# Counts of destinations taken ahead of the normalisation, and rank products placed behind 20 projection tiles instead of 30, in the sort stage of a graph-attention kernel

## Chip, cores and metric

The kernel runs on one core of a Trainium2 chip, as one program. The metric is the device time of one execution in microseconds (us). The kernel before takes 4097.71 us, the median of three runs (4089.75 to 4097.94).

## The reference, cut to what matters

Four layers run one after another over 6250 nodes and 106250 edges that come sorted by destination; the hidden width is 256.

```
x = x + gnn0(layernorm(x), src, dst, edge_attr)   # attention over edges, 8 heads
x = x + ffn0(layernorm(x))                        # sliced attention over nodes
x = x + gnn1(layernorm(x), src, dst)
x = x + moe(layernorm(x))                         # 8 experts, the best 2 for each node
```

The change touches only the stage ahead of the first layer. It finds where each node's edges begin in the sorted list (a count of the entries of `dst` below the node's number), orders the nodes by the number of their edges, and computes the first layer's projection of the normalised nodes, `layernorm(x) @ W.T` with 16 more columns of attention scores.

## The kernel before

`sort_nodes` is the first stage. Its 6250 nodes are 50 tiles of 125. Every engine has a list of instructions that it works off in order; engines wait for each other on semaphores. The stage ends with a barrier for all engines (the block begins at L259), and the next stage, `windows`, starts behind it.

**Counting, in two steps.** `dst` is cut into 250 blocks of 425 edges. TensorE counts for every node how many blocks begin below it (L518). `index(g)` (L349) turns the counts of 10 tiles into block numbers. GpSimd then gathers, tile by tile, the one block in which each node's first edge lies (L338): 125 rows of 425 integers, 212.5 KB, into a ring `drow` of R = 10 buffers. `count(t)` (L355) waits until gather t has landed, and counts the entries below each node; it frees the buffer (`used`). So gather t + 10 waits for `count(t)`, and for the `index` of its group of ten.

**VectorE's order (L358 to L399).** `index(0)`; a wait for the weights (`w_in`, L365); 25 tiles of the layernorm's statistics (`norm.tile`, L375); `index(1)` to `index(4)`; `count(0)` to `count(9)`; the other 25 statistics (L381); the variances; two copies that make the edge records `rec` (L385, L386); `norm.scales` (L388); `count(10)` to `count(49)`; then the starts of all nodes `rpf`, their degrees and a one-hot of the degrees, `hot` (L399).

**Projection, three engines and SyncE's queue.** For each tile ScalarE normalises (`xn`, L484), TensorE transposes (`turn`, L529) and multiplies (`product`, L538), ScalarE copies the result into one of RB = 5 buffers `row` (L496), and SyncE issues four DMAs that write it to `rows0` and `own0` (L282, L283). ScalarE's copy of tile t waits until tile t - 5 has been written. `product(t)` waits until row t - 2 has been copied. SyncE first waits for the edge records (`rec_made`, L268), writes them and four small zero rows, then issues 30 tiles, then a copy of the whole of `x` into `own0` (L288), then the other 20 tiles.

**Ranks.** `ranks()` (L547) is two products for each of 7 column blocks; VectorE copies each block out (L403, L404) before TensorE may write the next. TensorE's list is: ten tiles as `group(0)`, `group(1)`, `group(2)`, then `ranks()`, then `group(3)`, `group(4)`, then ten `place(g)` (L557), which need VectorE's one-hots `at_q`, `at_t` and `vals` (L423 to L427). Some small vector work on the result (L430 to L466) ends the stage.

Of the kernel before, what the change touches and what calls it, by code (L numbers as in the profile page):

```python
# [25 lines left out]
NT = N // P  # L26
# [136 lines left out]
def sort_nodes(nc, K, ins, dr):  # L163


    with ExitStack() as stack:
        m = Mem(nc, stack)
        J, R, RB, W, GT, PG, B = 2, 10, 5, 10, 10, 5, 2
# [90 lines left out]
        with nc.Block() as block:  # L259
# [85 lines left out]
            def _(dve):  # L345
# [3 lines left out]
                def index(g):  # L349
                    ts = slice(g * GT, (g + 1) * GT)  # L350
                    dve.wait_ge(counted, (g + 1) * GT)
                    v.tensor_scalar(blk_i[:, ts], pN[g], -1.0, 0.0, ALU.add, ALU.max).then_inc(idx_ok, 1)
                    v.tensor_scalar(blk[:, ts], pN[g], -1.0, 0.0, ALU.add, ALU.max)

                def count(t):  # L355
                    dve.wait_ge(landed[t % R], 16 * (t // R) + 16)
                    return v.tensor_scalar(drow[:, t % R, :], drow[:, t % R, :], node[:, t:t + 1], 0.0, ALU.is_lt, ALU.add, accum_out=cnt[:, t:t + 1]).then_inc(used, 1)
# [3 lines left out]
                for j in range(J):  # L361
                    v.tensor_scalar(below[:, j, :], iota_n, dst0f[:, j:j + 1], None, ALU.is_gt).then_inc(below_ok, 1)
                index(0)

                dve.wait_ge(w_in, 64)  # L365
                dve.wait_ge(consts, 3)
# [6 lines left out]
                half = NT // 2  # L373
                for t in range(half):
                    norm.tile(v, t, x[:, t:t + 1, :])  # L375
                for g in range(1, NT // GT):
                    index(g)
                for t in range(R):
                    count(t)
                for t in range(half, NT):  # L380
                    norm.tile(v, t, x[:, t:t + 1, :])  # L381
# [4 lines left out]
                v.tensor_copy(rec[:, :, 1:4], attrw[:]).then_inc(rec_made, 1)  # L386
                dve.wait_ge(sq, 1)
                norm.scales(v, ch, rst)  # L388
                for t in range(R, NT):
                    count(t)  # L390
                dve.sem_inc(used, 1)
                dve.wait_ge(used, NT + 1)
# [117 lines left out]
            @block.tensor  # L510
            def _(pe):
                t_ = nc.tensor
                bl = below[:].rearrange("p j (n t) -> p j t n", t=NT)
                pe.wait_ge(consts, 1)
                pe.wait_ge(below_ok, J)
                for t in range(NT):
                    for j in range(J):
                        last = t_.matmul(pN[t // GT][:, t % GT:t % GT + 1], bl[:, j, t, :], ones[:], start=(j == 0), stop=(j == J - 1))  # L518
                    last.then_inc(counted, 1)
                pe.wait_ge(ablk_ok, 1)  # L520
                for i in range(2):
                    for k in range(2):
                        last = t_.matmul(pW[:, i, 0:2 * H], wn[:, k, i * 128:(i + 1) * 128], ablk[:, k, :], start=(k == 0), stop=(k == 1))
                last.then_inc(wa_ok, 1)

                def turn(t, b):
                    pe.wait_ge(xn_ok, t + 1)
                    for k in range(2):
                        last = t_.transpose(pT[b][:, k, 0:P], xn[:, b, k * 128:(k + 1) * 128], K["ident"][0:P, 0:P])  # L529
                    last.then_inc(t_ok, 1)  # L530

                def product(t, b, early):
                    pe.wait_ge(xnT_ok, t + 1)
                    if not early:
                        pe.sem_inc(pace, 1)
                        pe.wait_ge(row_ok, t - 1)
                    for k in range(2):
                        last = t_.matmul(pH[b][:, 0:D + 2 * H], xnT[:, b, k, :], wx[:, k, :], start=(k == 0), stop=(k == 1))  # L538
                    last.then_inc(h_ok, 1)

                def group(u, first, last_group):
                    for r in range(W):
                        if r < W - 1 or not last_group:
                            turn(W * u + (r + 1), (r + 1) % 2)
                        product(W * u + r, r % 2, first and r < 2)

                def ranks():  # L547
                    pe.wait_ge(hot_ok, 1)
                    for j, (a, b) in enumerate(cols):
                        h = wide[:, a * NB:b * NB]  # L550
                        w = (b - a) * NB
                        if j:
                            pe.wait_ge(taken, j)
                        t_.matmul(pR[0:P, 0:w], K["tri"][0:P, 0:P], h, start=True, stop=True)
                        t_.matmul(pTt[:, 0:w], K["ones"][0:P, 0:P], h, start=True, stop=True).then_inc(mm_ok, 1)

                def place(g):  # L557
                    pe.wait_ge(hot2, g + 1)
                    for i in range(PG):
                        last = t_.matmul(pR[:, 0:3 * QT], at_q[:, g % B, i, :], vals[:, g % B, i, :, :].rearrange("p k t -> p (k t)"),  # L560
                                         start=(g == 0 and i == 0), stop=(g == NT // PG - 1 and i == PG - 1))
                    last.then_inc(placed, 1)
                pe.wait_ge(wx_ok, 1)
                turn(0, 0)
                group(0, True, False)
                group(1, False, False)
                group(2, False, False)
                ranks()
                group(3, False, False)
                group(4, False, True)  # L570
                for g in range(NT // PG):
                    place(g)
                pe.wait_ge(deg_ok, 1)
                t_.transpose(pD[0:QT, :], K["deg"][:], K["ident"][:]).then_inc(dT_ok, 1)
                pe.wait_ge(cnt_ok, 1)
                t_.matmul(pC[:, 0, 0:QT + 1], cf[:], K["tri"][0:QT, 0:QT + 1], start=True, stop=True)
                t_.matmul(pC[:, 1, 0:QT + 1], wf[:], K["tri"][0:QT, 0:QT + 1], start=True, stop=True)
                t_.matmul(pC[:, 1, QT + 1:QT + 2], none[:], K["ones"][0:QT, 0:1], start=True, stop=True)
                t_.matmul(pC[:, 1, QT + 2:QT + 3], shallow[:], K["ones"][0:QT, 0:1], start=True, stop=True)
                t_.matmul(pC[:, 2, 0:QT], c8[:], K["ident"][0:QT, 0:QT], start=True, stop=True)  # L580
                t_.matmul(pD[:, 0:QT], K["ones"][0:QT, :], diag[:], start=True, stop=True).then_inc(pre_ok, 1)
# [1600 lines left out]
```

## Time and profile before

| | |
|---|---|
| time, median of 3 runs (range) | 4097.71 us (4089.75 to 4097.94) |
| profiled execution: time | 4103.11 us |
| profiled execution: span, first to last instruction | 4101.4 us |
| busy share of the span: TensorE, VectorE, ScalarE, GpSimd | 73%, 56%, 31%, 56% |
| mean granted TensorE clock | 0.876 of full speed |
| end of the sort stage (the next stage's first instruction on GpSimd) | 238.67 us after the span's start |

The sort stage is the first 239 us of the span. The busy shares are averages over many stages with other limits, so what is said here is read from the stage's own stretch of the trace: the list of waits, the instructions in order of time, and the landing of transfers.

### The profile page before, as it was taken

To read this page: it belongs to the slowest core of one execution; us is meant where nothing else is said; L and a number is where in the kernel's file an instruction comes from. 1 tells how busy PE (TensorE), PEld (TensorE's weight loads), DVE (VectorE), ACT (ScalarE), POOL (GpSimd) and SP (SyncE) were. 2 spreads that over 40 slices of the span, in tenths; PEclk is the share of its full clock that TensorE was granted. 3 is DMA by queue.
4 is the path that set the end of the run, shared out by engine and by line. 5 is a ranking of instruction groups with operands and counts; after the bars stand their busy time and mean duration, and the time that the engine had idled before them with its cause. 6 is when DMAs were issued, how large, how long until landed. Compare 5 with 4: busy or idle time off the path is not lost. (4 is left out here: it accounts for less than half of the span.)

```text
span 4101.4 us, 69475 instructions
## 1 busy us (share of the span) xinstructions
PE 2992.8 (73%) x12787; PEld 2170.0 (53%) x12788; DVE 2302.0 (56%) x5192; ACT 1264.3 (31%) x5387; POOL 2289.2 (56%) x2343
## 2 busy tenths in 40 slices
PE   4632777787788777998666565566556489999998
PEld 3421444444444444667544444444444379998987
DVE  4532888888888887874355555555555621111111
ACT  1401444444445454432211111111111233433333
POOL 5156777777777773001477777777777523333332
PEclk9966899999999999998778877777787699999999
DMA  8636444344444443000244444444444756666664
GB/s 185 195 89 163 105 106 105 104 107 109 109 109 110 111 112 70 0 2 27 72 112 114 113 112 113 113 113 112 113 113 112 218 151 175 169 174 167 177 168 131
DMA packets 292185, 487.94 MB, mean 119 GB/s; under 512 B 145315, under 2 KB 193393, under 8 KB 291625
## 3 DMA queue, kind: packets, MB, share of 16 engines
q0 software_dynamic: 127312, 325.41, 32.3%
q1 hardware_dynamic: 155936, 158.55, 13.2%
q10 hardware_dynamic: 8880, 3.34, 0.4%
q8 instruction: 21, 0.34, 0.0%
q14 instruction: 36, 0.29, 0.0%
HBM read 430.09 MB, written 57.50 MB: 119 GB/s over the span
## 5 line engine op out<-in xcount | busy, mean ns | idle before, releaser
L893 POOL DMA_INDIRECT g_rows<-rows,g_recs x1856 | 1760.1, 948 | 643.3 <-issue 469.1
L933 PE MATMUL g_pA<-g_msg,k_ident 128*128 128x264 f32 (+1 forms) x3712 | 1140.7, 460 | 476.3 <-DVE g_pA L1122 418.9
L933 PEld LDWEIGHTS g_pA<-g_msg,k_ident 128*128 128x128 f32 x3712 | 800.0, 227 | 801.3 <-issue 659.5
L922 PE MATMUL g_pE<-g_ew,g_recT 128*128 128x512 f32 x932 | 508.6, 672 | 251.2 <-DVEq L1106 248.8
L1116 DVE TENSOR_TENSOR g_msg<-g_rows,g_pp 128x1024 f32 (+3 forms) x464 | 572.0, 1233 | 155.5 <-DVEq L84 155.4
L1962 POOL DMA_INDIRECT out<-e_ys,e_goal x102 | 160.6, 1575 | 490.5 <-issue 466.1
L922 PEld LDWEIGHTS g_pE<-g_ew,g_recT 128*128 128x128 f32 x932 | 169.8, 202 | 468.5 <-DVEq L1106 343.0
L2015 PE MATMUL e_pY<-e_w,e_hT 128*128 x1632 | 375.1, 383 | 19.5 <-issue 19.0
L2004 PEld LDWEIGHTS e_pH<-e_xT,e_w 128*128 128x128 f32 x3264 | 382.6, 193 | 5.1
L2004 PE MATMUL e_pH<-e_xT,e_w 128*128 128x128 f32 x3264 | 382.9, 276 | 0.0
L1041 ACT ACTIVATE g_pp<-g_dd 128x32 f32<-128x32 f32 x464 | 95.2, 205 | 919.3 <-ACTq L84 919.3
L2100 DVE TENSOR_TENSOR e_ys<-e_pY,k_x 128x256 f32<-128x256 f32 x102 | 43.4, 425 | 573.6 <-PE e_pY L2015 573.6
L2015 PEld LDWEIGHTS e_pY<-e_w,e_hT 128*128 128x128 f32 x1632 | 302.5, 190 | 68.9 <-issue 31.8
L1149 DVE TENSOR_REDUCE g_al<-g_prod 128x32 f32<-128x1088 f32 x232 | 297.1, 1281 | 56.4 <-DVEq L84 56.4
L1101 DVE SCALAR_TENSOR_TENSOR g_prod<-g_pE,g_dall 128x1024 f32<-128x1024 f32 x232 | 283.4, 1221 | 18.5 <-DVEq L84 7.3
L1055 ACT ACTIVATE g_pA<-g_pA,g_cs 128x33 f32<-128x33 f32 x1464 | 276.4, 277 | 4.4
L2057 ACT ACTIVATE e_hT<-e_pH,e_b 128x128 f32<-128x128 f32 x816 | 221.6, 382 | 43.1 <-issue 40.5
L2044 ACT ACTIVATE e_xT<-e_pX,e_bl,e_gl 128x128 f32<-128x128 f32 x204 | 82.2, 453 | 494.5 <-PE e_pX L1987 494.5
L994 ACT ACTIVATE g_recT<-g_pRT 16x128 f32<-16x128 f32 x234 | 62.2, 266 | 557.1 <-ACTq L84 556.9
L1153 DVE TENSOR_TENSOR g_al<-g_rows,k_sdst 128x32 f32 (+1 forms) x232 | 44.8, 193 | 287.1 <-DVEq L84 282.3
L1544 POOL MEMSET f_bu<- 128x16 f32 x1 | 0.1, 112 | 287.3 <-POOLq L113 287.3
L1949 POOL DMA_INDIRECT e_xs<-tok,e_at x102 | 100.4, 984 | 71.5 <-DVE e_at L2110 35.1
(418 smaller groups left out, 3467.6 us busy)
## 6 DMA issues: line engine op xcount, KB each, us to landing
e_w<-in_L_ffn_W SPq DMA_DIRECT2D x110, 1024.0 KB
g_rows<-rows,g_recs POOLq DMA_INDIRECT x1856
g_recs<-slots SPq DMA_DIRECT2D x468, 8.0 KB
tok<-e_xall SPq DMA_DIRECT2D x7, 910.0 KB
rows<-p_row SPq DMA_DIRECT2D x50, 119.0 KB
own<-p_row SPq DMA_DIRECT2D x50, 119.0 KB
p_x<-in_x SPq DMA_DIRECT2D x1, 5600.0 KB
own<-p_x SPq DMA_DIRECT2D x1, 5600.0 KB
```

Source lines behind the costliest of these rows:

```text
L893: pool.indirect_dma_start(out=rows[:, r, j, :], out_offset=None, in_=rows_d, in_offset=bass.IndirectOffsetOnAxis(ap=recs[:, r, 4 * j:4 * j ...
L922: last = t_.matmul(pE[:, c:c + 512], recT[:], ew[:].rearrange("p c d -> p (c d)")[:, c:c + 512], start=True, stop=True)
L933: last = t_.matmul(sums, K["ident"][:], of, start=False, stop=(j == C - 1), skip_group_check=True)
L1055: last = s.activation(of[:, h, :], of[:, h, :], ACT.Copy, scale=cs[:, h:h + 1])
L1101: v.scalar_tensor_tensor(to, pE[:].rearrange("p (c h w) -> p c h w", c=C, h=H), 0.0, over(by_head(own), 1, C), ALU.max, ALU.mult).then_inc ...
L1116: v.tensor_tensor(to, of, by, ALU.mult).then_inc(msg_ok, 1)
L1149: ch.link(v.reduce_sum(sc, prod[:], axis=AX))
L1949: pool.indirect_dma_start(out=xs[:, b, :], out_offset=None, in_=dr["tok"], in_offset=bass.IndirectOffsetOnAxis(ap=at[b][:, 0:1], axis=0)). ...
L1962: pool.indirect_dma_start(out=out, out_offset=bass.IndirectOffsetOnAxis(ap=goal_b[b][:, 0:1], axis=0), in_=ys[:, b, :], in_offset=None, bo ...
L2004: last = t_.matmul(pH[b][c][:, j, :], w1[:, b, k, units], xT[:, b, k, :], start=(k == 0), stop=(k == 1))
L2015: last = t_.matmul(pY[b][:], hT[:, b, k, :], w2[:, bass.ds(e, 1), k, :].rearrange("p a h -> p (a h)"), start=(k == 0), stop=(k == KC - 1))
L2057: last = s.activation(hT[:, b, c * HK + j, :], pH[b][c][:, j, :], ACT.Gelu, bias=b1[:, bass.ds(e, 1), c * HK + j])
```

## The change

VectorE's `index(1)` to `index(4)` and `count(0)` to `count(13)` go ahead of the wait for the weights, in four portions. `count(14)` to `count(23)` stand between the two halves of the statistics, where `count(0)` to `count(9)` stood. The rest, `count(24)` to `count(49)`, stays behind `norm.scales`. On TensorE `ranks()` goes ahead of `group(2)`. No instruction is added or taken away.

```diff
@@ -361,6 +361,16 @@
                 index(0)
+                index(1)
+                for t in range(4):
+                    count(t)
+                index(2)
+                for t in range(4, 7):
+                    count(t)
+                index(3)
+                index(4)
+                for t in range(7, 14):
+                    count(t)
 
                 dve.wait_ge(w_in, 64)
                 dve.wait_ge(consts, 3)
@@ -373,9 +383,7 @@
                 half = NT // 2
                 for t in range(half):
                     norm.tile(v, t, x[:, t:t + 1, :])
-                for g in range(1, NT // GT):
-                    index(g)
-                for t in range(R):
+                for t in range(14, 24):
                     count(t)
                 for t in range(half, NT):
                     norm.tile(v, t, x[:, t:t + 1, :])
@@ -386,7 +394,7 @@
                 norm.scales(v, ch, rst)
-                for t in range(R, NT):
+                for t in range(24, NT):
                     count(t)
@@ -564,8 +572,8 @@
                 group(0, True, False)
                 group(1, False, False)
+                ranks()
                 group(2, False, False)
-                ranks()
                 group(3, False, False)
                 group(4, False, True)
```

## Rows read from the trace of the kernel before

**Rows 1.** Waits in the sort stage: engine, line, waited for, us, times, longest.

```profile
ACT p_row L496 <- DMA own<-p_row: 45.8, 28, 10.0
DVE p_ablk L367 <- DMA p_wx<-in_L_gnn_WT: 31.1, 1, 31.1
DVE o_at_q L423 <- PE o_pR L560: 16.6, 1, 16.6
```

**Rows 2.** Waits of SyncE's own queue, sort stage.

```profile
SPq L270 <- DVE p_rec L386: 73.6, 1, 73.6
SPq L259 <- PEq L259: 13.3, 1, 13.3
```

**Rows 3.** TensorE in order of time: start, us, instruction.

```profile
121.26 1.15 PE L538 MATMUL o_pH<-p_wx,o_xnT 128*125 128x272 f32 x4
...
142.16 1.02 PE L554 MATMUL o_pR<-p_wide,k_tri 125*125 125x512 f32 x2
...
209.30 1.15 PE L538 MATMUL o_pH<-p_wx,o_xnT 128*125 128x272 f32 x4 [0.43 <-ACT o_xnT L489]
210.29 2.68 PE L560 MATMUL o_pR<-o_vals,o_at_q 125*128 125x147 f32 x20
```

**Rows 4.** SyncE's DMA issues in order of time.

```profile
113.83 0.32 SPq L282 DMA_DIRECT2D rows<-p_row  x1
...
131.89 0.32 SPq L282 DMA_DIRECT2D rows<-p_row  x1
...
151.64 0.32 SPq L282 DMA_DIRECT2D rows<-p_row  x1
...
153.68 16.49 SPq L288 DMA_DIRECT2D own<-p_x  x2
...
207.10 0.32 SPq L283 DMA_DIRECT2D own<-p_row  x1
...
222.74 0.32 SPq L283 DMA_DIRECT2D own<-p_row  x1
```

**Rows 5.** VectorE in order of time.

```profile
59.96 0.65 DVE L357 TENSOR_SCALAR_CACHE_REDUCE p_drow<-p_drow,p_node 125x425 int32<-125x425 int32 x1
...
65.72 8.25 DVE L135 BATCH_NORM_STATS2 p_st<-p_x 125x6 f32<-125x256 f32 x25
...
78.89 0.65 DVE L357 TENSOR_SCALAR_CACHE_REDUCE p_drow<-p_drow,p_node 125x425 int32<-125x425 int32 x1
...
131.04 0.66 DVE L357 TENSOR_SCALAR_CACHE_REDUCE p_drow<-p_drow,p_node 125x425 int32<-125x425 int32 x1 [1.02 <-DMA p_drow<-in_dst,p_blk_i]
...
135.62 3.49 DVE L399 TENSOR_TENSOR p_wide<-o_bkt,k_iota 125x3200 f32<-125x3200 f32 x1
...
194.71 0.41 DVE L426 TENSOR_TENSOR o_vals<-o_at_t,o_deg 125x245 f32<-125x245 f32 x1
```

**Rows 6.** GpSimd's gathers 3, 9, 10 and 49 in order of time.

```profile
24.42 1.21 POOL L338 DMA_INDIRECT p_drow<-in_dst,p_blk_i  x1 [0.30 <-issue]
...
33.45 1.21 POOL L338 DMA_INDIRECT p_drow<-in_dst,p_blk_i  x1 [0.30 <-issue]
61.52 1.20 POOL L338 DMA_INDIRECT p_drow<-in_dst,p_blk_i  x1 [26.86 <-DVE p_drow L357]
...
124.14 1.20 POOL L338 DMA_INDIRECT p_drow<-in_dst,p_blk_i  x1 [0.30 <-DVE p_drow L357]
```

**Rows 7.** DMA issues, gathers 3, 9 and 19 alone: last number us to landing.

```profile
p_drow<-in_dst,p_blk_i POOLq DMA_INDIRECT x1, 29.0
...
p_drow<-in_dst,p_blk_i POOLq DMA_INDIRECT x1, 23.9
...
p_drow<-in_dst,p_blk_i POOLq DMA_INDIRECT x1, 5.3
```

**Rows 8.** ScalarE's copy of tile 30, the first behind the ranks.

```profile
166.82 0.40 ACT L496 ACTIVATE p_row<-o_pH 125x272 f32<-125x272 f32 x1 [0.69 <-PE o_pH L538]
```

**Rows 9.** Windows: stretch, length, busy of PE, PEld, DVE, ACT, POOL, clock, DMA share, GB/s.

```profile
142.00:165.30 23.30, 12.46 (x30) 4.53 (x29) 10.29 (x12) 2.08 (x5) 0.00 (x0) 1.00 0.69 204
```

## The prediction

> **What bounds the kernel now.** The page's busy shares don't answer this: they are means over ten stages. The change lies in the sort stage, and the next stage starts behind a barrier, at 238.67 us. So the question is what ends the sort stage last, and I read its waits first, then the order of time on each engine that they point to.
>
> The waits hold two surprises. VectorE does sit idle for 31.1 us early on, until the weights land; but late in the stage it also waits 16.6 us for TensorE's placement products [rows 1]. VectorE had made the inputs of the first two placements by 195.12 (194.71 + 0.41) [rows 5], and TensorE began them only at 210.29, straight behind the product of tile 49, which started at 209.30 [rows 3]. The chain of counts therefore has 15 to 17 us to spare before the end: making it shorter makes that wait longer. The projection sets the end.
>
> What sets the projection? ScalarE's copies of the rows wait 45.8 us in 28 times for the writes of rows before them [rows 1], and those are issued by SyncE. Its queue hardly pauses: a tile takes four issues, 2.04 us from the last tile at 151.64 to the copy of x at 153.68, and the last write is issued at 222.74 [rows 4]. The list of its own waits has one long entry before it starts, the edge records (73.6 us), and one after it ends, 13.3 us at the barrier [rows 2]. Product 49 needs row 47, row 47's buffer needs tile 42 written, and tile 42's last issue is at 207.10 [rows 4], 2.2 us before the product. So the path is: the statistics and the records on VectorE, SyncE's queue to tile 42, product 49, placements, the small vector work. The stretch from the first placement to the barrier is 28.4 us (238.67 - 210.29) and does not change.
>
> Two questions are left. Does the change move the start of SyncE's queue? Does it make that queue run dry?
>
> **The early counts: the start.** The gathers that the early counts wait for share the transfer engines with the load of x. Gather 3, started at 24.42, took 29.0 us to land: 53.42 [rows 6, 7]. That hides now behind the wait for the weights, whose end lets the statistics start. In the changed order count 3 comes before that wait, and ten buffers bind everything that follows. Before, gather 10 started 1.56 us after the start of count 0 (59.96 to 61.52) [rows 5, 6]. So gather 13 starts at 53.42 + 1.56 = 54.98. GpSimd needs 1.505 us for each gather ((33.45 - 24.42) / 6 [rows 6]), so gather 23, ten later, starts at 54.98 + 15.05 = 70.03. Gather 19, issued when x had long landed, took 5.3 us [rows 7]; so gather 23 lands at 75.3. Count 23 stands ahead of the second half of the statistics, and a count takes 0.58 us (ten from 59.96 to 65.72 [rows 5]): that half starts at 75.9, where it started at 65.72. **Term 1: +10.2 us** for the second half and for all behind it: variances, records, scales, SyncE's first row.
>
> Nothing earlier on VectorE binds more tightly: gather 13 lands at about 60.3, so the weights' wait is reached at about 61, the first half of the statistics takes 8.25 us as the second does [rows 5], and counts 14 to 22 are taken as they land. The weights ended the old wait at about 51 (59.96 less 8.25 for the first half and about 1 for what lies around it), and could come ten us later without a change. Nor is the removal of the four `index` calls from their old place worth anything, as VectorE waits for gathers there.
>
> Bounds: if gather 3 landed as fast as gather 19, there would be no delay (a rival below); if it landed with gather 9, at 33.45 + 23.9 = 57.35 [rows 6, 7], the term would be 14.1.
>
> The Trainium skill (DMA: Bandwidth & Descriptors, "Anatomy of one DMA") puts a GpSimd-issued transfer at about 2.0 us plus its bytes over 436 GB/s. By that estimate gather 23's 212.5 KB would take 2.5 us, term 1 would be 7.4 and the sum 19.7; the trace's 5.3 us disagrees, and is used.
>
> **The ranks behind 20 tiles: the queue runs dry.** The ranks hold TensorE, and no row is made meanwhile. Before, they started at 142.16, behind tile 29, and the next row was written at 167.22 (166.82 + 0.40) [rows 3, 8], 25.06 us later. This stood where SyncE issued its stock of rows and then the copy of x, an issue of 16.49 us [rows 4]: the hole was covered. Behind tile 19 there is no such cover. In the clock of the old trace TensorE starts product 19 at 121.26; the product before the ranks started 0.99 us ahead of them (product 49 stood as far ahead of the placements [rows 3]), so ranks would start at 122.25 and row 20 would be ready at 147.31. SyncE was ready for tile 20 at 131.89 at the latest [rows 4]. **Term 2: 147.31 - 131.89 = +15.4 us** in which the queue stands still. It can't win that back: behind it lie the same thirty tiles and the copy of x.
>
> This adds to term 1, as both TensorE and SyncE are moved by it alike. Does TensorE wait for the one-hot as well? Count 24 starts where count 10 did, at 78.89 [rows 5], plus 10.2: 89.1. It frees gather 34 (89.1 + 1.56 = 90.65), and 15 more gathers start gather 49 at 113.2; with the last gather's 6.9 us (124.14 to 131.04) its count starts at 120.1, where it was 131.04. The one-hot ended 8.07 us after that start (135.62 + 3.49) [rows 5, 6]: 128.2. TensorE reaches the ranks at about 122.25 + 10.2 = 132.4, later. So no third wait, with some 3 us to spare.
>
> Bounds: below, TensorE alone needs 12.46 us for the ranks [rows 9], if VectorE's copies cost nothing: term 2 would be 25.06 - (23.30 - 12.46) - 9.64 = 4.6, where 9.64 is the stock (131.89 - 122.25). Above, if the last count came no earlier than 131.04, the one-hot would be ready at 139.1, 6.7 us after TensorE: 22.1. The middle value is taken, as the same instructions take the same turns.
>
> **What the gathers give back.** From 113.83 (tile 12) to 153.68, 18 tiles took 39.85 us; at the 2.04 us of the last of them they would take 36.7 [rows 4]. The gathers ran until 131 in that stretch. In the new order they have landed by 121, when tile 12 starts at about 124. **Term 3: -3.1 us**; the other bound is nothing.
>
> **Sum.** 10.2 + 15.4 - 3.1 = +22.5 us. The profiled execution's 4103.11 (span 4101.4 and 1.7 around it) becomes 4125.6. That execution is 5.4 us above the median of the runs, so on their footing it is 4097.7 + 22.5 = 4120.2, rounded to 4120, 0.55% slower. All later stages start behind the barrier and only shift.
>
> **The rivals.**
>
> *The count chain sets the end (faster).* The mechanism would be VectorE's: the last count comes 10.9 us sooner, so ranks and placements do. It decides if placements wait for VectorE and not for product 49. The new time would be 4097.7 - 10.9 = 4087, and SyncE's 13.3 us at the barrier would allow it [rows 2]. Against it stands the wait of 16.6 us in the other direction [rows 1]. 0.05.
>
> *It does nothing (same).* The early gathers land fast enough to leave the statistics where they are, and the hole in TensorE's rows is hidden by rows in stock. 4098. Against it: 29.0 us to land [rows 7] and five buffers, of which 9.64 us of issuing were left. 0.06.
>
> *Only the queue's hole.* Gathers 0 to 3 land early, term 1 is gone: 4097.7 + 15.4 - 3.1 = 4110. 0.06.
>
> *Only the late start.* ScalarE or TensorE is further ahead of SyncE at tile 20 than it was, and term 2 is gone or cut to its low bound: 4097.7 + 10.2 - 3.1 = 4105, or 4109 with the low bound's 4.6. 0.05.
>
> **How the numbers follow.** The forecast, both terms, has 0.78; its own range is 4112 to 4130: terms 1 and 2 together 8 us smaller, or 10 us larger, as with term 1 at its high bound (+3.9) and term 2 near its own (+6.7). The range that should hold 8 in 10 reaches down into the two half cases: 4107 to 4131. No change is what lies within 0.2%, 8.2 us, about what this kernel's runs can tell (their own spread is 8.2). Slower: 0.78 + 0.06 + 0.05 = 0.89; the same 0.06; faster 0.05.
>
> **What would show it.** In the new profile: the second half of the statistics starts near 76; SyncE's first issues come 10 us later; the ranks start near 132 and SyncE's issues stand still for about 15 us behind tile 19; the one-hot is ready a few us ahead of TensorE; VectorE's wait for the first placement grows from 16.6 us to some 50; the placements begin near 233 and the next stage near 262. I would be wrong if gather 3 landed long before 53, if SyncE's issues ran on behind tile 19, or if product 49 were no longer what the placements follow.

## The result and the profile after

The changed kernel takes 4118.46 us, the median of five runs (4116.0 to 4119.18), against 4094.72 for the kernel before (five runs, 4089.75 to 4097.94): a ratio of 1.0057, with a 95% interval of 1.0046 to 1.0068. It is 23.7 us slower; the forecast was 22.5.

The sort stage accounts for nearly all of it. The next stage begins on GpSimd at 260.86 us; before, it began at 238.67, so the stage is 22.2 us longer. The two profiled executions differ by only 12.9 us in span, 4114.3 against 4101.4: behind the sort stage the one of before took 3862.7 us and the one of after 3853.4, with the same work. The delay is not won back in the layers that follow: a load of the last layer on SyncE's queue (tile `e_br`) is issued at 3203.54 before and at 3227.05 after, still 23.5 us late. Only behind that is the execution of after 10.6 us shorter. The six experiments below took 3859.8 to 3863.1 us behind the sort stage, so the 3853.4 stands alone, and its cause is not known. The stage's own end and the timed medians are what to compare.

The waits of the stage come first: engine and line, what was waited for, us in total, times, longest. From the records on, the changed file's lines lie 8 further down.

```profile
ACT p_row L504 <- DMA own<-p_row: 56.3, 22, 27.5
DVE o_at_q L431 <- PE o_pR L568: 51.5, 1, 51.5
DVE p_drow L357 <- DMA p_drow<-in_dst,p_blk_i: 44.1, 21, 18.2
```

```profile
SPq L270 <- DVE p_rec L394: 85.2, 1, 85.2
...
SPq L259 <- PEq L259: 13.2, 1, 13.2
SPq L282 <- ACT p_row L504: 11.9, 1, 11.9
```

The second list is SyncE's own queue. Two entries answer to [rows 2]: the wait for the records grew from 73.6 to 85.2 us, and a wait of 11.9 us for a row is new. The 31.1 us that VectorE spent on the weights [rows 1] are gone from the list, but they are not filled with work: VectorE now waits there for the gathers instead (18.2 us ahead of count 0, 29.5 us in all up to count 13). Its waits for gathers were 27.2 us in the whole stage before, and are 44.1 now. The row of before:

```profile
DVE p_drow L357 <- DMA p_drow<-in_dst,p_blk_i: 27.2, 26, 4.7
```

Its wait for the placement products grew from 16.6 to 51.5 us: the chain of counts got shorter, and handed the time on to that wait.

VectorE in order of time shows the late start:

```profile
53.25 0.66 DVE L357 TENSOR_SCALAR_CACHE_REDUCE p_drow<-p_drow,p_node 125x425 int32<-125x425 int32 x1 [2.20 <-DMA p_drow<-in_dst,p_blk_i]
...
62.17 0.66 DVE L357 TENSOR_SCALAR_CACHE_REDUCE p_drow<-p_drow,p_node 125x425 int32<-125x425 int32 x1 [0.34 <-DMA p_drow<-in_dst,p_blk_i]
...
63.51 8.25 DVE L135 BATCH_NORM_STATS2 p_st<-p_x 125x6 f32<-125x256 f32 x25
71.68 0.64 DVE L357 TENSOR_SCALAR_CACHE_REDUCE p_drow<-p_drow,p_node 125x425 int32<-125x425 int32 x1
...
77.43 8.26 DVE L135 BATCH_NORM_STATS2 p_st<-p_x 125x6 f32<-125x256 f32 x25
...
124.79 3.49 DVE L407 TENSOR_TENSOR p_wide<-o_bkt,k_iota 125x3200 f32<-125x3200 f32 x1
```

Count 3 starts at 53.25, when gather 3 lands; count 13 at 62.17; only then does VectorE come to the weights, for which it no longer waits, and to the first half of the statistics. The second half starts at 77.43, 11.7 us later than in [rows 5].

SyncE's queue in order of time, tiles 0, 19 and 20 and the copy of x:

```profile
97.90 0.35 SPq L282 DMA_DIRECT2D rows<-p_row  x1
...
140.80 0.32 SPq L282 DMA_DIRECT2D rows<-p_row  x1
...
155.10 0.32 SPq L282 DMA_DIRECT2D rows<-p_row  x1
...
177.17 16.52 SPq L288 DMA_DIRECT2D own<-p_x  x2
```

Behind tile 19 there is a hole: a tile takes some 2.07 us, yet tile 20 is issued 14.3 us after tile 19. Against [rows 4] tile 20 and the copy of x are both 23 us late (23.2 and 23.5): nothing is won back. TensorE shows why the hole is there, and where it ends:

```profile
128.91 1.14 PE L546 MATMUL o_pH<-p_wx,o_xnT 128*125 128x272 f32 x4
129.89 1.02 PE L562 MATMUL o_pR<-p_wide,k_tri 125*125 125x512 f32 x2
...
153.27 1.08 PE L546 MATMUL o_pH<-p_wx,o_xnT 128*125 128x272 f32 x4
...
232.87 2.69 PE L568 MATMUL o_pR<-o_vals,o_at_q 125*128 125x147 f32 x20
```

Product 19, the ranks, then product 20 only at 153.27; the placements begin at 232.87, 22.6 us later than in [rows 3].

### The profile page after: what moved, and what is told of

Same layout as the page of the kernel before. It is cut to its first block and busy times, and to the rows that moved or that the text cites. A ratio compares the mean times of both kernels' runs of the same rounds, so it can differ in the third digit from the quotient of the medians.

```text
span 4114.3 us, 69475 instructions
## 1 busy us (share of the span) xinstructions
PE 2992.0 (73%) x12787; PEld 2168.0 (53%) x12788; DVE 2302.0 (56%) x5192; ACT 1267.3 (31%) x5387; POOL 2294.7 (56%) x2343
```

## Experiments

Theory: SyncE's queue of row writes sets the end of the stage. The early counts delay its start (term 1), the ranks behind 20 tiles let it run dry (term 2), and the two add. Rivals: only one of the two costs anything, or the chain of counts sets the end. Each experiment was timed in five rounds against the kernel before (median 4101.08 us in the first four, 4100.89 in the last two). That kernel took 4094.72 us beside the changed kernel, so between the two sets ratios and the stage's end are compared, not times. A stage's end, too, is that of one execution: in the profiles of the kernel before and of "the ranks alone", in which VectorE's order is the same, the statistics begin at 51.20 and at 49.55 us. In the fences, the `x_tailw` row is the next stage's first instruction on GpSimd, so its start is the stage's end.

**The early counts alone**

```diff
 # the changed kernel, with the ranks back in their place
-                ranks()
                 group(2, False, False)
+                ranks()
```

> The early counts alone, with the ranks behind 30 tiles as in the kernel before. Theory (two separate terms): the second half of the statistics starts near 77.4 us as in the changed kernel, SyncE's queue starts some 12 us late and never runs dry; the sort stage ends 9 to 12 us later than before, time +0.2 to +0.3%. Rival (all the loss comes from the ranks, VectorE's early waits are hidden): no difference, or a few us faster.

Measured: 4112.38 us, ratio 1.0029 (1.0018 to 1.0040). On VectorE, TensorE and GpSimd, in this order:

```profile
77.83 8.26 DVE L135 BATCH_NORM_STATS2 p_st<-p_x 125x6 f32<-125x256 f32 x25
...
153.06 1.02 PE L562 MATMUL o_pR<-p_wide,k_tri 125*125 125x512 f32 x2
...
249.52 0.21 POOL L668 MEMSET x_tailw<- 128x128 int32 x1 [126.42 <-POOLq L113]
```

The second half starts as late as in the changed kernel, the queue has no wait for a row, and the stage ends 10.9 us late. That is about half of the loss, and it has nothing to do with the ranks. The rival that VectorE's early waits are hidden falls.

**The ranks alone**

```diff
 # the kernel before
+                ranks()
                 group(2, False, False)
-                ranks()
```

> The ranks behind 20 tiles alone, with the counts as in the kernel before. Theory: TensorE reaches the ranks near 122 us, but the one-hot is ready only near 139, so the hole in the rows is longer than in the changed kernel: row 20 near 164 where SyncE is ready near 132, a dry queue for about 32 us, the stage ends about 31 us later, time +0.7 to +0.8%: more than both parts of the change together. Rival (the ranks cost a fixed hole of about 12 us wherever the counts are): +0.3%. Rival (the counts set the end): no difference.

Measured: 4133.82 us, ratio 1.0076 (1.0063 to 1.0090). TensorE, SyncE's queue, GpSimd:

```profile
135.59 2.07 PE L554 MATMUL o_pR<-p_wide,k_tri 125*125 125x512 f32 x2 [15.09 <-DVE p_wide L399]
161.90 0.48 PE L554 MATMUL o_pR<-p_wide,k_tri 125*125 125x128 f32 x2 [1.81 <-DVE p_wide L404]
...
SPq L282 <- ACT p_row L496: 34.5, 1, 34.5
...
269.93 0.21 POOL L660 MEMSET x_tailw<- 128x128 int32 x1 [139.84 <-POOLq L113]
```

The stage ends 31.3 us late, more than with both parts together: without the early counts the one-hot comes late, TensorE stands 15.09 us before the ranks, and the queue is dry for 34.5 us. That is 22.6 us more than in the changed kernel, but only 9.4 us of it are what the early counts give: row 20 is written at 164.32 here and at 154.94 there. The other 13.2 us are SyncE's, which is ready for tile 20 at 130.0 here and, with its late start, at 143.2 there. So the early counts do help the ranks; they only help a wait that the other part of the change has made. The rivals, a fixed hole of about 12 us (+0.3%) and no difference, fall.

**The copy of x moved along**

```diff
 # the changed kernel
-        UR = 3
+        UR = 2
```

> The changed kernel with SyncE's copy of x issued behind 20 tiles instead of 30, so that it stands again where TensorE makes no rows. Theory: the wait of 11.9 us in SyncE's queue goes, the early counts' late start stays: the stage ends 10 to 12 us later than in the kernel before, time +0.25%, some 12 us under the changed kernel. Rival (TensorE and not SyncE's queue is what the late ranks hold back): as the changed kernel, +0.57%.

Measured: 4113.55 us, ratio 1.0030 (1.0018 to 1.0041). SyncE's queue around tile 20, and the stage's end:

```profile
139.72 0.32 SPq L282 DMA_DIRECT2D rows<-p_row  x1
...
141.76 16.55 SPq L288 DMA_DIRECT2D own<-p_x  x2
158.67 2.24 SPq L282 DMA_DIRECT2D rows<-p_row  x1
...
247.75 0.21 POOL L668 MEMSET x_tailw<- 128x128 int32 x1 [126.12 <-POOLq L113]
```

The ranks stay behind 20 tiles, and the copy of x stands in the hole: no wait for a row is left in the queue's list, and the stage ends 9.1 us late instead of 22.2, a little less than the 10 to 12 expected (the first half of the statistics began at 62.77 in this execution, 0.7 us sooner than in the changed kernel's). What ranks at this place cost is the cover that they lost.

**All statistics first**

```diff
 # the kernel before; VectorE's order behind index(0):
+                for g in range(1, NT // GT):
+                    index(g)
+                dve.wait_ge(x_in, 32)
+                for t in range(NT):
+                    norm.tile(v, t, x[:, t:t + 1, :])
                 dve.wait_ge(w_in, 64)
...
-                for t in range(half):
-                    norm.tile(v, t, x[:, t:t + 1, :])
-                for g in range(1, NT // GT):
-                    index(g)
-                for t in range(R):
-                    count(t)
-                for t in range(half, NT):
-                    norm.tile(v, t, x[:, t:t + 1, :])
...
                 norm.scales(v, ch, rst)
-                for t in range(R, NT):
+                for t in range(NT):
                     count(t)
```

> The kernel before with VectorE's order turned the other way: all five index calls, then all 50 tiles of statistics as soon as x has landed, then the weights, the variances, the records and the scales, and all 50 counts behind them; ranks behind 30 tiles. Theory (the start of SyncE's queue sets the end): if x has landed by about 35 us the statistics end near 51, the records near 57 instead of 78, and the stage ends about 20 us sooner (14 to 22), time -0.5%. Rival (the chain of counts sets the end): the last count comes only about 7 us sooner, so at most -0.17%. If x lands only near 50 us: about -6 us.

Measured: 4088.31 us, ratio 0.9968 (0.9956 to 0.9979). VectorE, TensorE, SyncE's queue, GpSimd:

```profile
38.36 16.43 DVE L135 BATCH_NORM_STATS2 p_st<-p_x 125x6 f32<-125x256 f32 x50 [0.36 <-DMA p_x<-in_x]
...
57.23 0.91 DVE L380 COPY p_rec<-p_srcw 125x850 int32<-125x850 int32 x1
...
132.16 3.49 DVE L394 TENSOR_TENSOR p_wide<-o_bkt,k_iota 125x3200 f32<-125x3200 f32 x1
...
135.71 2.07 PE L549 MATMUL o_pR<-p_wide,k_tri 125*125 125x512 f32 x2 [9.67 <-DVE p_wide L394]
...
SPq L282 <- ACT p_row L491: 15.5, 1, 15.5
...
226.89 0.21 POOL L655 MEMSET x_tailw<- 128x128 int32 x1 [96.92 <-POOLq L113]
```

x lands at about 38 us, so the same idle stretch holds all the statistics, and the records are begun at 57.23 instead of 75.73. The stage ends 11.8 us sooner. The direction is the theory's; the size is not (14 to 22 were expected). The one-hot comes only at 135.65, TensorE waits 9.67 us for it, and the queue runs dry for 15.5 us: with an early start the chain of counts becomes a bound after all. It does not set the end alone: by that rival at most 0.17% could be won, and the interval's least gain is 0.21%.

**Three counts early**

```diff
 # the kernel before
                 index(0)
+                index(1)
+                for t in range(3):
+                    count(t)
...
-                for g in range(1, NT // GT):
+                for g in range(2, NT // GT):
                     index(g)
-                for t in range(R):
+                for t in range(3, R):
                     count(t)
```

> The kernel before with only index(1) and counts 0 to 2 ahead of the wait for the weights; the ranks stay behind 30 tiles. Theory (what the early counts cost is the landing of the gathers, and only of those that land behind the weights): counts 0 to 2 are done by about 51 us, when the weights land, so the first half of the statistics starts where it did (within 1 us), the second half 1.5 to 2 us sooner for the three counts that it no longer waits for; the stage ends 0 to 2 us sooner, time within 0.1% of before. Rival (each early count costs its share of the changed kernel's 11.7 us): about 2.5 us later.

Measured: 4101.09 us, ratio 0.9996 (0.9987 to 1.0005): no difference. The statistics' halves on VectorE, the first half of the kernel before and then both of this one:

```profile
51.20 8.25 DVE L135 BATCH_NORM_STATS2 p_st<-p_x 125x6 f32<-125x256 f32 x25
...
49.96 8.26 DVE L135 BATCH_NORM_STATS2 p_st<-p_x 125x6 f32<-125x256 f32 x25
...
62.60 8.26 DVE L135 BATCH_NORM_STATS2 p_st<-p_x 125x6 f32<-125x256 f32 x25
```

The first half is not held back: it starts 1.2 us before the 51.20 of the profiled kernel before. Count 2 began at 48.69, and behind it VectorE had no wait for the weights: in this execution they had landed by 49.3, where they came at 50.55 in the profile of before. The second half starts 3.1 us before its place in [rows 5], the other 1.9 us for the three counts, and one `index`, that are gone from between the halves. So early counts cost next to nothing here, where their gathers land about when the weights do; each costing its share, 2.5 us in all, falls. The stage ends at 234.76, 3.9 us sooner, a little more than was expected; as executions differ by some 1.7 us in when the statistics begin, and the time shows no gain, no more than "no loss" is shown.

**All statistics first, 25 buffers**

```diff
 # the experiment "All statistics first"
-        J, R, RB, W, GT, PG, B = 2, 10, 5, 10, 10, 5, 2
+        J, R, RB, W, GT, PG, B = 2, 25, 5, 10, 10, 5, 2
...
+        slot = lambda r: drow[:, r, :] if r < 10 else wide[:, (r - 10) * EJ:(r - 9) * EJ].bitcast(I32)
... (the gathers and the counts use slot(t % R) in place of drow[:, t % R, :])
```

> The order with all statistics first, with 25 buffers for the gathers in place of 10 (15 of them in the tile that later holds the one-hot). Theory: with statistics first SyncE's queue ran dry for 15.5 us because the one-hot came only at 135.7 us; with 25 buffers GpSimd has 25 gathers out before the first count frees one, the last gather starts near 99 us instead of 121, the one-hot is ready near 114, ahead of TensorE's tile 29 near 124, the dry wait goes and the stage ends near 220 us (238.7 before, 226.9 with ten buffers): time -0.4 to -0.5%. Rival (the queue's start and the x copy set the end alone): the stage stays at 227, -0.3%. Rival (more gathers out while x loads delay x and the weights): the statistics start later than 38.4 us and the gain shrinks.

Measured: 4084.04 us, ratio 0.9961 (0.9947 to 0.9975). VectorE, TensorE, SyncE's queue, GpSimd:

```profile
38.96 16.43 DVE L135 BATCH_NORM_STATS2 p_st<-p_x 125x6 f32<-125x256 f32 x50 [0.95 <-DMA p_x<-in_x]
...
113.71 3.49 DVE L395 TENSOR_TENSOR p_wide<-o_bkt,k_iota 125x3200 f32<-125x3200 f32 x1
...
125.64 1.02 PE L550 MATMUL o_pR<-p_wide,k_tri 125*125 125x512 f32 x2
...
SPq L283 <- ACT p_row L492: 5.7, 8, 3.1
...
222.54 0.21 POOL L656 MEMSET x_tailw<- 128x128 int32 x1 [110.85 <-POOLq L113]
```

The one-hot is ready at 117.2, ahead of TensorE; the ranks start behind product 29 without a wait, and the stage ends 16.1 us sooner than before, 4.4 us sooner than with ten buffers, where some 7 were expected. The 15.5 us of dry queue are gone, but eight short waits for rows, 5.7 us in all, have come: with more gathers in flight a copy that waits for its row buffer starts 8 to 10 us after the last issue of that buffer's write until the gathers are over, where it was mostly 4 to 5 us with ten buffers. (The statistics start 0.6 us later than with ten. Three of the fifteen more gathers had been issued by then, so this says little of what all fifteen would do to x.) This version beats both kernels; that it is faster than the one with ten buffers, its time alone does not establish, as their intervals overlap.

## Why the prediction was right, and where its terms were off

**What sets the end: right.** The placements followed product 49 again, at 232.87 ("near 233"). VectorE's wait grew to 51.5 us ("some 50"). The rival in which the count chain sets the end would have been faster; the one-hot did come 10.8 us sooner (128.28 against 139.11), and the kernel got slower.

**Term 1, +10.2 forecast, +11.7 measured.** Count 3 came when it was said to (53.25 against 53.42). But the step "nothing earlier on VectorE binds more tightly" was wrong. By the prediction's own numbers it was a tie: the weights' wait at 61, about 1 around it, 8.25 for the first half and ten counts of 0.58 come to 76, against the 75.9 that it took from gather 23. GpSimd started gathers 13 and 23 at 54.20 and 69.30, and the view of DMA issues has their times to landing, in this order:

```profile
54.20 1.21 POOL L338 DMA_INDIRECT p_drow<-in_dst,p_blk_i  x1 [1.66 <-DVE p_drow L357]
...
69.30 1.21 POOL L338 DMA_INDIRECT p_drow<-in_dst,p_blk_i  x1 [0.30 <-issue]
```

```profile
p_drow<-in_dst,p_blk_i POOLq DMA_INDIRECT x1, 7.9
...
p_drow<-in_dst,p_blk_i POOLq DMA_INDIRECT x1, 4.8
```

Gather 13, issued while those before it were still landing, took 7.9 us where 5.3 were assumed, and count 13 started at 62.17. That put the first half at 63.51, and the ten counts behind it ran from 71.68 without a pause: not gather 23 but the first half's late start set the second. Gather 23 had landed by 74.1, ahead of its count at 76.86. The estimate of 2.5 us from the Trainium skill's figure (DMA: Bandwidth & Descriptors, "Anatomy of one DMA") is not what these transfers take here either; the measured 4.8 and 7.9 decide.

That the first gathers share the engines with the load of x is only part of why they land late. In "all statistics first", whose loads and first ten gathers are issued alike, x was in by 38.4 us; gather 3 of the kernel before landed at 53.4. In the last of that time, from 46 us on, the gathers' own queue had 87% of the transfer engines' time and the queue that loads x 3%. Why ten gathers then need so long, no run shows.

**Term 2, +15.4 forecast, a wait of 11.9 us measured.** The mechanism, the place and the ranks' length held: from the ranks' start at 129.89 to the end of ScalarE's copy of row 20 (154.54 + 0.40) it was 25.05 us, where the forecast had 25.06. What was mis-sized is the stock. Product 19 came at 128.91, only 7.65 us later than in [rows 3], while the queue's tile 19 came 11.3 us later than before: TensorE was further ahead of SyncE, 11.9 us instead of 8.2, where the prediction had both "moved by it alike". The buffers of the rows came free sooner. Here is the last issue of tile 13's write and the copy of tile 18, which waits for that write, before and after:

```profile
117.47 0.32 SPq L283 DMA_DIRECT2D own<-p_row  x1
122.31 0.40 ACT L496 ACTIVATE p_row<-o_pH 125x272 f32<-125x272 f32 x1 [1.20 <-DMA own<-p_row]
...
128.24 0.32 SPq L283 DMA_DIRECT2D own<-p_row  x1
129.63 0.40 ACT L504 ACTIVATE p_row<-o_pH 125x272 f32<-125x272 f32 x1 [0.87 <-DMA own<-p_row]
```

It was 4.84 us before and 1.39 after. In the other traces it is the same: 4 to 6 us as long as gathers land (8 to 10 with 25 buffers), mostly 1.4 us behind the last count, whether that comes at 110, 121 or 131 us. So the gathers' earlier end gave TensorE its lead.

**Term 3, -3.1 forecast.** This term's mechanism is not borne out: the gathers hardly slow SyncE's issues. With the early counts alone, where no hole lies in it, the stretch from tile 12 to the copy of x took 39.3 us (125.28 to 164.57) against 39.85, a gain of 0.6. In the changed kernel the queue gained 0.7 us from tile 0 to tile 19, and from tile 20 to the end of the stage about 1 us. What the gathers gave back was TensorE's lead over SyncE, and so it went into term 2. Terms 2 and 3 together are 10.9 us (22.6 at the placements less 11.7), where 12.3 were forecast. So the errors, +1.5 in term 1 and -1.4 in the other two, cancelled: that the sum came within about 1 us is luck. That the queue starts late and then runs dry is not.

**That the terms add.** Taking the second term away, by the place of the ranks or by that of the copy of x, leaves 10.9 and 9.1 us of the 22.2: that is the first. The two parts of the change do not add in the same way: alone, the early counts cost 10.9 us and the late-placed ranks 31.3. The forecast's ranks' term already counts on a one-hot that the early counts have brought forward, and on a SyncE that they have held back.

## What to carry to other kernels

Filling an engine's idle time with instructions that themselves wait can delay what follows in its list: what belongs into such a gap is work whose inputs are there, and the one whose output the longest queue is waiting for (here the statistics, not the counts). A stretch in which one engine makes nothing for another is free only where the consumer has other work in its queue; if one of the two is moved, the other has to move too. And before shortening a chain, look at who waits at its end: a wait of 16.6 us there said that nothing could be gained by that alone.

## What the runs showed of the hardware

TensorE's pause before the ranks cost more than its length. In both experiments in which it stood idle for 9.7 to 15.1 us before them, its clock in the windows view fell; columns are the stretch, its length, busy time of PE, PEld, DVE, ACT and POOL, the granted clock, the DMA share and GB/s. First the experiment with all statistics first, ten buffers:

```profile
135.00:142.00 7.00, 4.48 (x5) 1.65 (x6) 2.37 (x3) 0.00 (x0) 0.00 (x0) 0.50 0.94 281
142.00:150.00 8.00, 6.19 (x8) 1.82 (x6) 1.72 (x2) 0.00 (x0) 0.00 (x0) 0.50 1.06 318
```

then the ranks alone, and the changed kernel:

```profile
135.00:142.00 7.00, 4.61 (x5) 1.65 (x6) 2.25 (x3) 0.00 (x0) 0.00 (x0) 0.50 0.00 0
...
135.00:142.00 7.00, 3.39 (x8) 1.15 (x7) 3.43 (x4) 0.27 (x1) 0.00 (x0) 1.00 0.44 130
```

At 0.50, the 1.2 GHz level, the first product of 512 columns takes 2.07 us instead of 1.02, with the transfer engines busy (0.94) or idle (0.00) alike. From the first rank product to the last pair it was 28.1 us with all statistics first (135.71 to 163.83) and 26.3 us with the ranks alone, against 22.6 us at 2.4 GHz (142.16 to 164.79 before). The difference lies in the first pairs of products, three of them in the one and two in the other: from one pair's start to the next it is 5.6 us at the low level and 3.8 at the high one. Of the 15.5 us for which the queue ran dry with all statistics first, 9.67 are thus TensorE's wait and about 5.5 the low clock behind it. A pause as long as these is not needed: in the kernel before the granted clock was 0.50 from 125 to 130 us, behind a wait of 3.2 us ahead of tile 20.
